# Reciprocal roots of the layer and group norms as one GpSimd power operation each

## The reference, cut to what matters

```python
def _ln_c(v, eps=1e-6):                 # _ln_t: the same on tokens, eps=1e-5
    m = jnp.mean(v, axis=1, keepdims=True)
    s = jnp.var(v, axis=1, keepdims=True)
    return (v - m) / jnp.sqrt(s + eps)

x = x + _L0_conv_ref(_ln_c(x), ...)     # 1x1 to 576 channels, silu, 3x3 depthwise, silu, gate, 1x1 to 96
t = t + _L0_ffn_ref(_ln_t(t), ...)      # 96 -> 384 -> 96, quantised to fp8 and fp16
x = x + _L1_conv_ref(_ln_c(x), ...)     # conv1, group_norm1, gelu, 4 shifted convs with gelu, group_norm1, conv3
t = t + _L1_ffn_ref(_ln_t(t), ...)

def group_norm1(x, gamma, beta):        # one mean and one variance for a whole image
    mean = jnp.mean(x, axis=(1, 2, 3), keepdims=True)
    var = jnp.var(x, axis=(1, 2, 3), keepdims=True)
    xn = (x - mean) * jax.lax.rsqrt(var + EPS)
    return xn * gamma[None, :, None, None] + beta[None, :, None, None]
```

## Time and profile before

| | |
|---|---|
| time, median of 3 runs | 6618.72 us (6617.19 to 6633.22) |
| profiled execution: span from the first to the last instruction | 6626.1 us (the page gives no other time for it) |
| instructions | 158187 |
| PE busy | 5391.3 us (81%) |
| DVE busy | 5443.2 us (82%), 8976 instructions |
| ACT busy | 4404.2 us (66%) |
| POOL busy | 478.0 us (7%), 366 instructions |
| granted TensorE clock, mean | 0.958 of full speed |

### The profile page before, as it was taken

The page is one execution under the profiler, slowest core; times in us unless marked ns, Lnnn a source line. Parts: engine busy times, 40 slices in busy tenths (PEclk is TensorE's granted clock), DMA queues, the critical chain, the costliest instruction groups (busy, mean ns, idle before and its releaser), DMA issues.

```text
span 6626.1 us, 158187 instructions
## 1 busy us (share of the span) xinstructions
PE 5391.3 (81%) x63744; PEld 2286.2 (35%) x63744; DVE 5443.2 (82%) x8976; ACT 4404.2 (66%) x7673; POOL 478.0 (7%) x366
## 2 busy tenths in 40 slices
PE   1788888888888888888888888888888888888875
PEld 0333333333333333333333333333333333333331
DVE  4788988888988888888888888888888888888863
ACT  1466766667766766766667766667766766766754
POOL 1000000000000000000000000000000000000000
PEclk9899999999999999999999999999999999999987
DMA  1233323333323433423333423333423433333322
GB/s 42 65 79 88 97 68 91 97 82 90 98 72 88 101 79 89 98 70 89 98 80 89 99 70 88 99 81 89 99 73 88 99 79 90 97 78 85 88 67 58
DMA packets 395662, 559.44 MB, mean 84 GB/s; under 512 B 71490, under 2 KB 391427, under 8 KB 391771
## 3 DMA queue, kind: packets, MB, share of 16 engines
q1 hardware_dynamic: 394940, 549.32, 33.4%
HBM read 233.66 MB, written 78.68 MB: 47 GB/s over the span
## 4 chain that ended last, share of the span: by engine, by line
PE 43%; DVE 32%; ACT 12%; issue 6%; SPq 3%; DMA 3%; ACTq 0%; DVEq 0%
PE bank L522 25%; DVE conv L874 19%; PE b_banks L522 6%; ACT hidden L790 3%; PE bank L575 3%; PE bank L562 2%; PE b_banks L678 2%; PE sums_b L529 2%; DVE hidden L930 2%; DMA r_b<-rstd_row_b 2%; ACT hidden L797 2%; DVE bn_stats L945 1%; DVE x L940 1%; DVE xn L922 1%; ACT mid L730 1%
## 5 line engine op out<-in xcount | busy, mean ns | idle before, releaser
L874 DVE SCALAR_TENSOR_TENSOR conv<-mid,w_dw,conv 128x1568 f32<-128x1568 f32 x1536 | 2893.7, 1884 | 18.2
L522 PE MATMUL bank<-x,centering 128*32 128x392 f32 x6144 | 884.6, 509 | 227.2 <-DVE b_q L1105 102.7
L522 PE MATMUL bank<-conv,w_proj_gated 128*32 128x392 f32 x7680 | 879.1, 493 | 0.0
L522 PE MATMUL bank<-xc_a,w_exp 128*32 128x392 f32 x6144 | 730.8, 511 | 158.8 <-DVE xc_a L857 57.6
L678 PE MATMUL b_banks<-shifted,w_combo 128*32 128x392 f32 x6144 | 651.4, 546 | 251.3 <-DMA shifted<-g 152.7
L790 ACT ACTIVATE hidden<-b_banks 128x1176 f16<-128x1176 f32 x512 | 589.4, 1151 | 341.1 <-PE b_banks L522 338.9
L797 ACT ACTIVATE hidden<-hidden 128x1176 fp8e5<-128x1176 f16 x512 | 607.6, 1187 | 29.9 <-DVE hidden L930 29.7
L706 ACT ACTIVATE g<-bank 96x392 f32<-96x392 f32 x512 | 253.6, 495 | 561.7 <-PE bank L522 410.1
L1017 POOL TENSOR_TENSOR x<-x,xc_a 96x392 f32<-96x392 f32 x256 | 458.5, 1802 | 1760.3 <-DVE xc_a L857 1760.3
L522 PE MATMUL b_banks<-xn,w_q 128*32 128x392 fp8e5 x6144 | 490.1, 336 | 65.7 <-DVE xn L922 46.5
L730 ACT ACTIVATE mid<-bank 128x392 f32<-128x392 f32 x768 | 379.2, 498 | 211.6 <-PE bank L522 209.8
(11 more groups left out here) (170 smaller groups left out, 7691.3 us busy)
## 6 DMA issues: line engine op xcount, KB each, us to landing
phases_on<-phases SPq DMA_DIRECT2D x768, 101.5 KB, 2.6
shifted<-g SPq DMA_DIRECT2D x512, 149.6 KB, 2.7
r_b<-rstd_row_b SPq DMA_DIRECT2D x512, 147.0 KB, 3.0
shifted<-g SPq DMA_DIRECT2D x256, 199.5 KB, 3.0
x<-in_x SPq DMA_DIRECT2D x32, 1176.0 KB, 8.0
r_a<-rstd_row_a SPq DMA_DIRECT2D x256, 147.0 KB, 3.3
x_plus_norm<-x SPq DMA_DIRECT2D x256, 147.0 KB, 2.7
r_a<-x_plus_norm SPq DMA_DIRECT2D x256, 147.0 KB, 2.4
```

The costliest lines, as they stand in the source:

```text
L522: last = mm(o[j:j + QUAD, :], weights[:, j:j + QUAD], x, start=start, stop=stop)
L874: v.scalar_tensor_tensor(out=acc, in0=src, scalar=WDW[:, k, j:j + 1], in1=acc, op0=ALU.mult, op1=ALU.add).then_inc(sem["convolved"], 1)
```

## The change

The nine DVE instructions of each reciprocal root go. One GpSimd instruction raises the variance to the power -0.5, with the exponent from a constant array `minus_half` that a tenth memset of GpSimd's setup fills. DVE still computes the variance plus eps, and signals it; GpSimd waits for that signal, SP and PE for what they waited for before with the counts of the shorter sequences. In the group norms DVE waits for GpSimd's root before it goes on.

GpSimd's table gets the steps `rstd_a`, `rstd 0`, `rstd 1`, `rstd 2`, `root 0` and `root 1`, each 30 units behind DVE's step, and its `norm_a` and `gn 0` get numbers 60 units behind DVE's. Its order in one period is then: `rstd 1`, `root 0`, `gn 0` (memsets), `rstd_a`, `norm_a` 0 to 6, `root 1`, `norm_a` 7, `rstd 2`, `rstd 0`. The order on the other engines is the same as before.

```diff
-        "norm_a": (23011, 23065, 23501, 23724, 23746, 24366, 24606, 24671), "gn 0": (35382,)},
+        "norm_a": (5003, 5361, 5380, 5673, 5733, 6416, 6469, 7258), "gn 0": (24055,),
+        "rstd_a": (4250,), "rstd 0": (19994,), "rstd 1": (22621,), "rstd 2": (27666,), "root 0": (24025,), "root 1": (27103,),
+    },
...
-    TMP = {th: sb(f"newton_{th}", [VT * QUAD, VW], fp32) for th in "ab"}
+    HALVED = sb("minus_half", [128, VW], fp32)
...
-            v.tensor_scalar(V[bufs][:, :], VPS[th], 1.0 / C, eps, ALU.mult, ALU.add).then_inc(sem[s], 1)
-            vector_seed(Y[bufs][:, :], V[bufs][:, :], s, 3 * q)
-            dve.wait_ge(sem[s], at(3 * (q + 1)))
-            vector_newton(Y[bufs][:, :], V[bufs][:, :], TMP[bufs][:, :], f"rstd_{th}", NEWT * q)
+            v.tensor_scalar(V[bufs][:, :], VPS[th], 1.0 / C, eps, ALU.mult, ALU.add)\
+                .then_inc(sem[f"seed_{th}"], 1)
...
-                vector_seed(col(GY), col(GV), "gn_vector", base + 4)
-                dve.wait_ge(sem["gn_vector"], at(base + GN_V))
-                vector_newton(col(GY), col(GV), col(GT), "gn_rstd", NEWT * q)
-                dve.wait_ge(sem["gn_rstd"], at(NEWT * (q + 1)))
+                dve.wait_ge(sem["gn_rstd"], at(q + 1))
...
+        def root(th, bufs):
+
+            g.tensor_tensor(Y[bufs][:, :], V[bufs][:, :], HALVED[:, :], ALU.pow).then_inc(sem[f"rstd_{th}"], 1)
+
...
+            elif name == "rstd_a":
+                pool.wait_ge(sem["seed_a"], at(n + 1))
+                root("a", "a")
+            elif name == "rstd":
+                L = arg[0]
+                if L == 0:
+                    pool.wait_ge(sem["seed_c"], at(a + 1))
+                    root("c", "a")
+                else:
+                    pool.wait_ge(sem["seed_b"], at(2 * b + L))
+                    root("b", "b")
+            elif name == "root":
+                pool.wait_ge(sem["gn_vector"], at(GN_V * (2 * b + arg[0] + 1)))
+                g.tensor_tensor(GN[:, GY:GY + 1], GN[:, GV:GV + 1], HALVED[0:C, 0:1], ALU.pow)\
+                    .then_inc(sem["gn_rstd"], 1)
```

More of the change, by code:

```diff
@@ L1 @@
-import math
 import concourse.bass as bass
@@ L37 @@
 QUAD = 32
-SEEDS, NEWT = 3, 7
-RSQRT_SEED = float(0x5F3759DF - 2 * (1 << 23) - (1 << 31))
-ROOT_K = math.sqrt(0.75)
 EPS_BN, EPS_LNC, EPS_LNT, EPS_GN = 1e-3, 1e-6, 1e-5, 1e-5
@@ L133 @@
 }
-WHOLE = ("load_x", "rstd_a", "rstd", "se1", "se2", "se3", "gn", "gn_weights")
+WHOLE = ("load_x", "rstd_a", "rstd", "se1", "se2", "se3", "gn", "gn_weights", "root")
 USES_RING = ("center_a", "center", "expand", "texp", "tconv", "se1", "se2", "proj", "down", "fold")
@@ L285, in program @@
     N_SHIFT = 5
-    GN_V, GN_P = 7, 3
+    GN_V, GN_P = 5, 3
     def at(count):
@@ L341, in wait_sums @@
         if name == "var_a":
-            pe.wait_ge(sem["seed_a"], at(3 * (i + 1) + 1))
+            pe.wait_ge(sem["seed_a"], at(i + 2))
         elif a[0] == 0:
-            pe.wait_ge(sem["seed_c"], at(3 * i + 1))
+            pe.wait_ge(sem["seed_c"], at(i + 1))
         else:
-            pe.wait_ge(sem["seed_b"], at(3 * (2 * (i - 1) + a[0] - 1) + 1))
+            pe.wait_ge(sem["seed_b"], at(2 * (i - 1) + a[0]))
     def wait_bank(pe, prev):
@@ L374, in wait_bank @@
             pe.wait_ge(sem["layer0_done"], at(NT * i + a[0] + 1))
[L377 to L410, removed]
     def sync_steps(sp):
         def rstd_out(th, bufs, count):
-            sp.wait_ge(sem[f"rstd_{th}"], at(NEWT * count))
+            sp.wait_ge(sem[f"rstd_{th}"], at(count))
             dram = var_dram[th]
@@ L837, in seed @@
             dve.wait_ge(sem[f"varsummed_{th}"], at(NT * (q + 1)))
-            dve.wait_ge(sem[f"rstd_{th}"], at(NEWT * q))
+            dve.wait_ge(sem[f"rstd_{th}"], at(q))
             dve.wait_ge(sem[f"rstd_stored_{th}"], at(16 * VT * q))
-            s = f"seed_{th}"
-            v.tensor_scalar(V[bufs][:, :], VPS[th], 1.0 / C, eps, ALU.mult, ALU.add).then_inc(sem[s], 1)
-            vector_seed(Y[bufs][:, :], V[bufs][:, :], s, 3 * q)
-            dve.wait_ge(sem[s], at(3 * (q + 1)))
-            vector_newton(Y[bufs][:, :], V[bufs][:, :], TMP[bufs][:, :], f"rstd_{th}", NEWT * q)
+            v.tensor_scalar(V[bufs][:, :], VPS[th], 1.0 / C, eps, ALU.mult, ALU.add)\
+                .then_inc(sem[f"seed_{th}"], 1)
         for i, (name, *arg), bank, _ in plan["DVE"]:
@@ L1034, in program @@
              (b2_raw, w["b2"])]
-    n_pool_setup = 9
+    n_pool_setup = 10
     rv, ry, rt = (ACC[2][:, 256 * n:256 * n + NCK + 1 + C] for n in range(3))
@@ L1121, in setup_gpsimd @@
         g.memset(Hm[1][:, :], 0.0).then_inc(sem["setup_pool"], 1)
+        g.memset(HALVED[:, :], -0.5).then_inc(sem["setup_pool"], 1)
         pool.wait_ge(sem["setup_pool"], n_pool_setup)
```

## The result

| | before | changed |
|---|---|---|
| median of 4 runs | 6620.86 us | 8354.01 us (8344.99 to 8356.72) |
| ratio | 1 | 1.2608, 95% interval 1.2588 to 1.2628 |
| span of the profiled execution | 6626.1 us | 8353.6 us |

A forecast was written before the change was run, and what follows sets the result against it. PE and DVE, each busy four fifths of the span, alternate on the chain, so DVE savings count only there. Gains of 1.7 + 0.5 = 2.2 us an image, 70 us in 32, gave 6549 us; 8-in-10 range 6490 to 6770.

The forecast's parts named there:

- the price of the added instruction: P, the time of GpSimd's 128x98 power in each layer norm: 2 us taken, range 0.35 to 7 us.
- What is removed: DVE's root instructions: 2.57 us a layer norm, 1.70 a group norm, 13.7 us an image, 438 us in 32 images.
- The 96x1 power: Group norm's root on GpSimd: 0.4 us (bounds 0.1 and 1.7), 0.56 with both hops, making `gn 0` 1.1 us earlier.
- The sum's 1.7 us "gain" at that wait: From `gn 0` to the last depthwise step: DVE 2.0 us earlier, gain capped by ACT's 1.7 us wait per image.
- The hold on DVE: A power blocks DVE's two-input instructions for P - 0.35 = 1.65 us in each of three layer norms.
- The dependence on P: Each microsecond of P costs one at `rstd 0` and, over 2.3, one at `rstd_a`; no change at P = 3.2.
- near 15: Expected sign: ACT's total wait for DVE's last depthwise step falls from 67 us to near 15.
- The slack: Room for later roots: 1.5 us at `rstd 2`, three convolution steps at `rstd 1`, SP's store 1.4 us after DVE at `rstd_a`.
- a root later by 2 us would be felt: Warning at `rstd 1`, from DVE's waits for these rows of 61.4 us in 69 instances; no gain or loss counted there.
- Rival 3: Slow power, P from 3.5 us: late roots, SP stuck before `shift 1`, DVE shut out; 6650 to 6900 us, chance 0.33.
- The sum for P = 7: Against P = 5, 2 us more at each of four places: given as 6.4 to 8 us an image, over 6900.
- The chances: Stated odds: faster 0.51, same 0.17, slower 0.32; the forecast itself (6520 to 6590 us) 0.35.

The follow-up runs named there:

- e1: Changed kernel with only the two group norms' roots as GpSimd powers, layer norms' roots back on DVE: 6601.0 against 6611.5 us before, ratio 0.9983.
- e4: Changed kernel with layer-norm powers cut to 12 of 98 columns, other roots left at 1.0: 6553.3 us, ratio 0.9908 to the kernel before.
- e3: Changed kernel with layer-norm powers cut to 24 of 98 columns, other roots left at 1.0: 6710.3 us, ratio 1.0150 to the kernel before.
- e8: Changed kernel with only the root of `rstd 2` as a GpSimd power, all others on DVE: 7056.0 against 6613.05 us before, ratio 1.0662.
- e5: Changed kernel with only the root of `rstd_a` as a GpSimd power, all others on DVE: 7019.8 against 6613.05 us before, ratio 1.0607.

## Why the prediction was wrong

**The step that failed is the price of the added instruction:** "I take P = 2 us, eight element operations", with 7 us as the upper bound. It is 16.04 us: 0.160 us a column where the add has 0.0026, which is sixty-two times as much, not eight (the value taken) or twenty-seven (the upper bound). The bound was worked out from a count of operations that no row of the trace showed. It looked like a bound and was a guess; with no row for the operation, no row of another kind could bound it from above.

**The rest of the sum, by its own steps.**
- *What is removed* is right: 2.57 us a layer norm and 1.70 a group norm; of the 438 us forecast 60 are gaps between 1728 instructions (0.035 us each), the other 378 were to go from DVE's busy time, and 362 went.
- *The 96x1 power* is 0.55 us for the 0.4 taken, and DVE's part of the group norm 0.81 us between variance and gain for the 0.56 + affine step taken: right within its bounds. Its gain was put too high: DVE is 1.07 us an image earlier, ACT's wait for the last depthwise step stays (63.9 us in e1 against 67.2), and 10 us came of it. The sum's 1.7 us "gain" at that wait is so not shown by any run as it was meant.
- *The hold on DVE* (P - 0.35) is wrong. The rows of the add show it, the power does not have it: six depthwise steps take 11.29 us beside a power and 11.28 without. The Trainium skill (SBUF — State Buffer, section "Who interferes with whom") lets the holder keep the shared ports for the whole instruction; for a power the measurement differs, and decides. What stays is the power's own 1.5 us behind a depthwise step.
- *The dependence on P* is right where it could be tried. At P = 2 the sum said 6549 us, and e4 with 2.27 us took 6553.3; its break-even of P = 3.2 is 3.0 on the line between e4 and e3; a straight line between its values for 3.2 and 5 gives 75 to 106 us of loss at e3's 4.16, and 98.8 were measured. That it is so close is partly luck: the hold on DVE that it charged does not exist, the gain at ACT's wait is smaller (42.1 us are left of it in e4, 29.9 in the changed kernel, where "near 15" was forecast), and where e4's 58 us come from instead was not taken apart.
- *The slack* was partly misread. At `rstd 1` the warning that "a root later by 2 us would be felt" is right: 0.2 us at the norm. At `rstd 2` the 1.5 us come from a piece of the chain that starts at 3253.79; PE's timeline has the first matmul of `up 1` at 3252.79, 0.5 us behind the norm, and e8 hides 0.6. At `rstd_a` SP's 1.4 us are 1.5 in e5, and another 1.6 are hidden between the store and the norm.
- *Rival 3* named what happened: late roots, and SP standing in its store before `shift 1`. Its shutting out of DVE did not happen, and its price, 6650 to 6900, rested on the same bound. The sum for P = 7 is wrong by itself as well: 2 us more at each of four places are 8 us on top of 4.4 to 6.2, so 12.4 to 14.2 us an image and 7015 to 7073 us, not "6.4 to 8, over 6900". The same rule carried on to 16.04 gives 4.4 to 6.2 + 4 x 11.04 = 48.6 to 50.4 us an image, 8170 to 8230 us; measured 8354. The chances, too, sum to 0.50 for faster and 0.33 for slower, not 0.51 and 0.32.

The four places add up to 1774 us, what the four powers add to 1833 us (57.3 us an image). The norms behind them come 51 us an image later, 1630 us; so the loss is the power's length, four times an image, less some 6 us of slack, plus a rest of about 140 us for which the slower clock is the candidate.

## What to carry to other kernels

An operation that the trace does not show has no upper bound from a count; where the sum crosses zero within what it might cost, time the one instruction by itself first, at two widths: the line through them gives the price, and the width at which the change pays. Look for a shape in which it is cheap: here the one-column roots pay on GpSimd and the 98-column ones do not, and e1, with the group norms alone, is the one version with every root computed that beats the kernel before, by 0.17%. And count slack from where the data land, not from the steps between producer and consumer in one engine's order: three steps of 5.6 us stood between `rstd 1` and its norm, and the way through HBM took 5.3 of them.

## What the runs showed of the hardware that I had not expected

- GpSimd's power is 0.160 us a column of 128 partitions and 0.35 us to start; only one in four of the partitions holds roots here, and whether fewer partitions or a shape of fewer columns would cost less was not tried. DVE's work beside it cost it 1.5 us at most (17.6 us against 16.04).
- The matrix engine's clock fell. Windows of the changed kernel around the power of `rstd 2`, and of the kernel before in the same place (columns: stretch, length, busy us of PE, PEld, DVE, ACT, POOL with counts, granted clock, DMA share, GB/s):

```profile
4304.00:4320.00 16.00, 15.38 (x192) 6.90 (x189) 8.43 (x11) 8.51 (x20) 0.00 (x0) 1.00 0.11 35
4320.00:4342.00 22.00, 10.14 (x93) 3.58 (x87) 4.82 (x5) 0.88 (x2) 16.06 (x1) 0.84 0.07 22
4342.00:4358.00 16.00, 15.88 (x204) 7.76 (x207) 13.56 (x24) 10.44 (x16) 0.00 (x0) 0.90 0.37 83
```

```profile
3228.00:3244.00 16.00, 15.38 (x192) 6.88 (x189) 8.44 (x12) 8.51 (x20) 0.00 (x0) 1.00 0.11 31
3244.00:3252.00 8.00, 8.00 (x78) 2.97 (x74) 6.52 (x12) 0.88 (x2) 0.00 (x0) 1.00 0.19 60
3254.00:3270.00 16.00, 16.00 (x220) 7.65 (x217) 13.61 (x26) 12.30 (x18) 0.00 (x0) 1.00 0.38 92
```

PE finishes its projection, then idles 12 us for the roots, and the clock is partly at the lower of its two levels (1.2 GHz against 2.4) in that stretch and in the one behind it, where PE has work again: 204 matmuls in 16 us where 220 had been. In finer stretches the granted clock is 1.00 up to 4334, PE having stopped at 4330, 0.50 from 4338 to 4342, and 0.60 from 4342 to 4346, where PE is back with 30 matmuls in 4 us; the next 4 us have 63, at 1.00. Over the span the mean clock is 0.867 against 0.958, and the same 63744 matmuls are busy 5588.6 us against 5391.3. How much of these 197 us lies on the path was not tried. The table of e5 to e8 leaves 0.8 to 1.5 us an image at each place above the norm's delay, some 140 us in all, which bounds it roughly.
